# Causal attentions: q and k as 32-row fp32r strips instead of bf16 parts copied through DRAM

## What is computed

```
qkv = x @ W;  att = q k^T / 4;  att = where(causal, -1e9, att)
out = softmax(att) @ v @ W_out                      # sublayers 0 and 4
scores = (q k^T) * tril;  out = softmax(scores / 32) @ v @ Wo   # sublayer 6
```

## Time and profile before

| | us |
|---|---|
| runs | 1302.36, 1304.68, 1298.7 |
| profiled execution, span | 1298.8 |
| PE busy | 1006.1 (77%) |
| DVE busy | 816.7 (63%) |
| ACT busy | 472.6 (36%) |
| POOL busy | 253.6 (20%) |
| largest group, maxima on DVE (L954, 576) | 284.3 |
| largest on PE, scores for maxima (L1374, 576) | 182.2 |

### The profile page before, as it was taken

One profiled execution on the slowest core, in us unless ns is written; L12 is line 12 of the kernel. 1 busy time (PEld: TensorE's weight loads), 2 busy tenths in 40 slices (PEclk: granted clock), 3 DMA queues, 4 the chain that ended last, 5 costly groups with the idle time before them and its releaser, 6 DMA issues.

```text
span 1298.8 us, 16170 instructions
## 1 busy us (share of the span) xinstructions
PE 1006.1 (77%) x5870; PEld 561.0 (43%) x5870; DVE 816.7 (63%) x1958; ACT 472.6 (36%) x1041; POOL 253.6 (20%) x378
## 2 busy tenths in 40 slices
PE   5469998789137877689999645999967469999785
PEld 3124443674125554443736421444444124443575
DVE  4558883767139999453232635888768468885566
ACT  1115565431038876221011110555612104557232
POOL 4000000333028776200000300000198000000033
PEclk8669999889659897689999975999967669999788
DMA  7950000101580000020000197200001970000000
GB/s 261 153 69 2 2 2 1 33 1 23 108 175 22 1 2 1 1 96 1 1 0 1 49 146 97 99 2 2 2 0 49 152 91 2 2 2 1 1 1 33
DMA packets 18907, 54.69 MB, mean 42 GB/s; under 512 B 2065, under 2 KB 3633, under 8 KB 17804
## 3 DMA queue, kind: packets, MB, share of 16 engines
q1 hardware_dynamic: 18828, 53.65, 20.9%
HBM read 40.90 MB, written 12.45 MB: 41 GB/s over the span
## 4 chain that ended last, share of the span: by engine, by line
PE 51%; DVE 29%; issue 10%; DMA 5%; ACT 4%; SPq 1%; POOL 1%; DVEq 0%; POOLq 0%; ACTq 0%
PE bank L1284 8%; PE bank L1374 8%; PE pair L1284 6%; PE pvb L1418 6%; DVE pmx L954 5%; PE pair L1401 5%; PE bank L1622 4%; DVE nm L1077 3%; PE bank L1576 3%; DMA scratch<-parts 3%; ACT PB L698 2%; PE pair L1289 2%; DVE PB L1089 2%; DVE rest L1192 2%; DMA QO<-scratch 2%
## 5 line engine op out<-in xcount | busy, mean ns | idle before, releaser
L954 DVE TENSOR_REDUCE pmx<-bank 128x1 f32<-128x512 f32 (+3 forms) x576 | 284.3, 551 | 121.8 <-PE bank L1377 94.7
L698 ACT ACTIVATE PB<-pair 128x1024 f32<-128x1024 f32 (+3 forms) x288 | 225.0, 812 | 289.1 <-PE pair L1404 246.3
L1374 PE MATMUL bank<-KO,QO 96*128 96x512 bf16 (+3 forms) x576 | 182.2, 366 | 66.8 <-issue 51.0
L1401 PE MATMUL pair<-QO,KO 99*128 99x512 bf16 (+3 forms) x576 | 152.9, 332 | 33.1 <-issue 31.1
L1374 PEld LDWEIGHTS bank<-KO,QO 96*128 96x128 bf16 x576 | 55.3, 101 | 205.2 <-DVE pmx L954 100.1
L1418 PE MATMUL pvb<-PB,V 128*32 128x512 f32 (+3 forms) x1152 | 124.0, 501 | 0.0
L1487 PE MATMUL pair<-KO,QO 96*128 96x192 bf16 x256 | 60.5, 280 | 75.8 <-DMA QO<-scratch 48.9
L735 ACT ACTIVATE KO<-pair,nm 128x192 f32<-128x192 f32 x216 | 87.8, 422 | 79.3 <-DVE nm L1077 77.5
L577 POOL TENSOR_TENSOR QO_r<-rest,acc 128x512 fp32r<-128x512 f32 x16 | 21.3, 1332 | 462.5 <-DVE acc L1198 462.5
L1077 DVE TENSOR_REDUCE nm<-pair 128x2 f32<-128x384 f32 x128 | 65.0, 545 | 48.7 <-PE pair L1489 48.1
L836 DVE TENSOR_TENSOR X<-bank,X 128x256 f32<-128x256 f32 x56 | 23.7, 423 | 105.4 <-PE bank L1622 43.9
(11 more groups left out here) (216 smaller groups left out, 1726.6 us busy)
## 6 DMA issues: line engine op xcount, KB each, us to landing
scratch<-parts SPq DMA_DIRECT2D x14, 768.0 KB, 11.8
QO<-scratch SPq DMA_DIRECT2D x36, 256.0 KB
KO<-scratch SPq DMA_DIRECT2D x36, 256.0 KB
WF<-in_moe_gu SPq DMA_DIRECT2D x1, 3520.0 KB, 27.9
WA<-in_w_att SPq DMA_DIRECT2D x3, 1024.0 KB, 10.6
QO<-scratch SPq DMA_DIRECT2D x24, 128.0 KB
WF<-in_tern_w SPq DMA_DIRECT2D x1, 3072.0 KB, 10.2
V<-in_moe_d SPq DMA_DIRECT2D x1, 1792.0 KB, 8.5
```

Of the source, the lines that this page charges most:

```text
L698: act.activation(pb[:, st % 2, 2 * i:2 * i + 2, 0:n], ps[:, :, 0:n], ACT.Exp, scale=scale)\
L954: r_done(dve.tensor_reduce(pmx[:, g % 2, c, t, j:j + 1], ps[:, 0:n], AX.X, ALU.max))
L1374: last = pe.matmul(ps[:, 0:n], q_op[0:KROWS, h, t * P:(t + 1) * P], k_op[0:KROWS, h, c * HALF:c * HALF + n], start=True, stop=not diag)
L1401: last = pe.matmul(ps[:, j, 0:n], k_op[0:KROWS + 3, h, kb * P:(kb + 1) * P], q_op[0:KROWS + 3, h, q0:q0 + n], start=True, stop=not diag)
```

## The change

q and k are no longer split in bf16 parts. The weights of q and k arrive with each head's 16 columns doubled (`both`), so that the projection gives 32 rows per head, four heads on 128 partitions. q becomes one strip per head: rows 0 to 15 the value rounded to fp32r, rows 16 to 31 the rest (two ScalarE copies with scales from `strip_sv`, and a subtraction on POOL, which makes the sign come out). k becomes two operands, the rounded value and its rest, each in both halves. A score is two fp32r matmuls over 32 rows. The maximum, in two fp32r terms, is added by a third one against ones. Everything stays in SBUF; `replicate`, `maxima` and their DMAs are gone for the causal attentions. There are 16 projections of 512 columns per attention instead of 8, spread over the plan ("k", "q" items).

The causal mask leaves TensorE: for the maxima VectorE adds it while it reduces (`maximum`), for the exponentials POOL sets the forbidden triangle of exp(scores) to zero (`causal_half`), and the product with V waits for it. Maxima are now computed two heads at a time; such a pair can ride in an "exp" item, on the other two strips, its matmuls between those of the exponentials. `HEAD_START` counts 10 items, pairs now. The transposes of the maxima go to a double bank and ScalarE copies them. The ternary weights of the last sublayer are prepared on POOL partly between its new work.

```diff
-HEAD_START = 18
+HEAD_START = 10
 def max_units(g, qh):
 
-    units = [(("max", g, t, c, j), 60 + min((t + 1) * P - c * HALF, HALF))
-             for t in range(qh * TH, (qh + 1) * TH) for c in range(1 + qh) for j in range(HG)]
-    return units + [(("m", g, qh), 600)]
+    units = [(("max", g, t, c, jj), 2 * (60 + min((t + 1) * P - c * HALF, HALF)))
+             for t in range(qh * TH, (qh + 1) * TH) for c in range(1 + qh) for jj in range(2)]
+    units.append((("m", g, qh), 600))
+    n = len(STAGES)
+    k = STAGES.index((g, qh)) + 1
+    if 1 < k < n:
+        at = len(units) // 2
+        units[at:at] = [((side,) + STAGES[k], 0) for side in ("k", "q")]
...
+    plan = [("k", 0, 0), ("q", 0, 0)] + [("v", t) for t in range(TH)] + [("x1",), ("k", 0, 1), ("q", 0, 1)] \
+        + [("v", t) for t in range(TH, NT)]
     ahead = [(item, cost, n) for n, stage in enumerate(STAGES) for item, cost in max_units(*stage)]
...
@@ -186,11 +200,17 @@
                     for m in range(len(STAGES)) if ahead and m >= ahead[0][2]], default=0)
         for i in range(2):
             lead += rate / 2
+            if i == 0 and g == 0:
+                plan += [("suffix", t) for t in (NT - 1 - 2 * k, NT - 2 - 2 * k) if t >= 0]
+            with_exp = None
+            if ahead and lead > 0 and ahead[0][0][0] == "max":
+                if ahead[1][0][0] == "max" and ahead[0][0][4] == i and ahead[0][0][:4] == ahead[1][0][:4]:
+                    ahead[0], ahead[1] = ahead[1], ahead[0]
+                with_exp, cost, _ = ahead.pop(0)
+                lead -= cost
+            plan.append(("exp", g, qh, kb, i, with_exp))
             while ahead and lead > 0:
                 lead -= take()
-            if i == 0 and g == 0:
-                plan += [("suffix", t) for t in (NT - 1 - 2 * k, NT - 2 - 2 * k) if t >= 0]
-            plan.append(("exp", g, qh, kb, i))
             if (g, qh, i) == (NG - 1, 1, 1):
...
+            def causal_half(s, item):
+
+                _, g, qh, kb, i, _ = item
+                pool.wait_ge(e_free, e_after(s, item))
+                p2 = pb[:, STEP[g, qh, kb] % 2, 2 * i:2 * i + 2, 0:P]
+                pool.affine_select(p2, p2, pattern=[[0, 2], [1, P]], compare_op=ALU.is_ge, fill=0.0, base=0,
+                                   channel_multiplier=-1).then_inc(causal, 1)
+
+            def strip(s, n, item):
+
+                side, g, half = item
+                cols = slice(half * HALF, (half + 1) * HALF)
+                pool.wait_ge(e_free, e_after(s, item))
+                if side == "q":
+                    ins = pool.tensor_tensor(qs[:, g, cols], y_f[:, n % 2, :], h_r[:, n % 2, :].bitcast(F32), ALU.subtract)
+                else:
+                    ins = pool.tensor_tensor(ks[1][:, g, cols], y_f[:, n % 2, :], ks[0][:, g, cols].bitcast(F32),
+                                             ALU.subtract)
+                ins.then_inc(strip_ready, 1)
+
...
+                    if item[0] in ("k", "q"):
+
+                        side, g, half = item
+                        cols = slice(half * HALF, (half + 1) * HALF)
+                        ps = e_slot()[:, 0, :]
+                        if strips >= 2:
+
+                            act.wait_ge(strip_ready, strips - 1)
+                        y = y_f[:, strips % 2, :]
+                        if side == "q":
+                            act.activation(y, ps, ACT.Copy, scale=strip_sv[:, 0:1])
+                            act.activation(h_r[:, strips % 2, :], ps, ACT.Copy, scale=strip_sv[:, 1:2]).then_inc(e_free, 1)
+                        else:
+                            act.activation(y, ps, ACT.Copy)
+                            act.activation(ks[0][:, g, cols], ps, ACT.Copy).then_inc(e_free, 1)
+                        strips += 1
+                    if item[0] == "mT":
 
                         _, g, qh = item
-                        ts = slice(qh * TH, (qh + 1) * TH)
-                        act.wait_ge(mp_ready, 2 * (NG * a + g) + qh + 1)
-                        act.activation(em[:, g % 2, ts, :], nm[:, g % 2, ts, :], ACT.Exp, scale=scale)\
...
+            def maximum(g, t, c, j):
+
+                n = min((t + 1) * P - c * HALF, HALF)
+                ps = r_slot()
+                to = pmx[:, g % 2, c, t, j:j + 1]
+                if (t + 1) * P - c * HALF <= HALF:
+                    r_done(dve.tensor_tensor_reduce(junk[:, (r_used - 1) % 3, 0:n], ps[:, 0:n], tri[:, HALF - n:HALF], 1.0, LOWEST,
+                                                    ALU.add, ALU.max, accum_out=to))
+                else:
+                    r_done(dve.tensor_reduce(to, ps[:, 0:n], AX.X, ALU.max))
 
...
-                        dve.wait_ge(mrow_ready, n + 1)
-                        dve.nop().then_inc(r_free, 1)
+                            dve.wait_ge(e_free, e_after(s, ("mT",) + STAGES[n - 2]))
+                        top, low = (nms_r[:, n % 2, :, k:P:STRIP] for k in range(2))
+                        step(dve.tensor_copy(top, nm[:, b, ts, :]))
+                        dve.tensor_tensor(low, nm[:, b, ts, :], top.bitcast(F32), ALU.subtract).then_inc(mp_ready, 1)
                     if item[0] == "accT":
                         _, g, qh = item
                         t0 = qh * TH
...
+                        unit = item if item[0] == "max" else item[5]
+                        if unit:
+                            _, gm, t, c, jj = unit
+                            if (c, t % TH, jj) == (0, 0, 0):
+                                pe.wait_ge(strip_ready, len(STRIPS) * a + STRIPS.index(("q", gm, t // TH)) + 1)
+                            nx = min((t + 1) * P - c * HALF, HALF)
+                            px = [r_slot()[:, 0:nx] for _ in range(2)]
+                        if item[0] == "exp":
+                            _, g, qh, kb, i, _ = item
+                            if kb == i == 0:
+
+                                pe.wait_ge(e_free, e_after(s, ("mT", g, qh)))
+                                if (s, g, qh) == (0, 0, 0):
+                                    pe.wait_ge(v_blank, 2)
+                            q0, n = span(qh, kb)
+                            b = STAGES.index((g, qh)) % 2
+                            ps = e_slot()
+                        for part in range(3):
+                            for j in range(2 if item[0] == "exp" else 0):
+                                if part < 2:
+                                    last = scores(ps[:, j, 0:n], ks[part][:, g, kb * P:(kb + 1) * P], qs[:, g, q0:q0 + n],
+                                                  2 * i + j, part == 0, False)
+                                else:
+                                    rows = slice((2 * i + j) * STRIP, (2 * i + j) * STRIP + 2)
+                                    at = q0 - qh * HALF
+                                    last = pe.matmul(ps[:, j, 0:n], ones_r[rows, :], ms[rows, b, at:at + n],
+                                                     start=False, stop=True)
+                            if part == 2 and item[0] == "exp":
+                                last.then_inc(e_full, 1)
+                                e_at[g, qh, kb] = e_used
+                            for j in range(2 if unit and part < 2 else 0):
+                                last = scores(px[j], qs[:, gm, t * P:(t + 1) * P], ks[part][:, gm, c * HALF:c * HALF + nx],
+                                              2 * jj + j, part == 0, part == 1)
+                                if part:
+                                    last.then_inc(r_full, 1)
                     if item[0] == "pv":
                         _, g, qh, kb = item
                         st = STEP[g, qh, kb]
...
 
                             pe.wait_ge(acc_ready, ACC0[s] + 2 * g + qh)
                         pe.wait_ge(e_free, e_at[g, qh, kb])
+                        if (g, qh, kb, 1) in DIAGS:
+                            pe.wait_ge(causal, len(DIAGS) * a + DIAGS.index((g, qh, kb, 1)) + 1)
                         for j in range(HG):
                             last = pe.matmul(pvb[j * STRIP:(j + 1) * STRIP, q0 - qh * HALF:HALF],
...
     down = np.concatenate([g["L1_ffn_down_w"].transpose(0, 2, 1).reshape(-1, D), g["L1_ffn_sh_down_w"].T,
                            np.zeros((NF_MOE * P - F_MOE, D), np.float32)], 0)
+
+    def both(wq, wk):
+
+        w = np.stack([chunks(w).reshape(P, ND, NG, HG, HD) for w in (wq, wk)], 1)
+        w = w.transpose(0, 3, 1, 2, 4, 5)
+        return np.ascontiguousarray(np.broadcast_to(w[:, :, :, :, :, None, :], (P, NG, 2, ND, HG, DUP, HD))
+                                    .reshape(P, NG, 2, ND, P))
+
+    w0, w2 = g["L0_attn_w_project"].T, g["L2_attn_w_qkv"]
...
```

363 lines of the change are left out of this document (166 added, 197 removed).

## The result

| | before | after |
|---|---|---|
| median of four runs, us | 1300.5 | 1500.1 (1478.0 to 1513.3) |
| ratio, 95% interval | | 1.146, 1.136 to 1.157 |
| profiled execution, span | 1298.8 | 1476.3 |
| mean granted clock | 0.866 | 0.796 |
| PE busy | 1006.1 | 1187.5 |

The kernel is 15% slower. The ratio leaves out the two runs of after that took over 1.5% more than its fastest one (1500.3 and 1513.3), so it is smaller than the quotient of the medians. The prediction, 1290 us in a range of 1240 to 1352, was wrong. The rest became 91.6 us shorter, as forecast; the third phases became 269 us longer where 85.5 were forecast.

A forecast was written before the change was run, and what follows sets the result against it. DMA and latency were taken to bound the first two phases, TensorE the third. -98 + 3 x 28.5 = -12.5 us on the 1298.8 span gives 1286.3; the median lies 3.6 higher, so 1290, range 1240 to 1352.

The forecast's parts named there:

- third phases: Each causal attention from its first exponential step on, bound by TensorE; forecast to grow by 28.5 us each.
- Phases one and two: Projection, then first maxima, before the first exponential step of each causal attention: 98 us saved in all, bounds 85 to 110.
- The strips run together: Third phase: matmuls on different strips of 32 rows were assumed to run with full concurrency, a 512 column round costing 0.23 us.
- the rival of strips in turn: Third phase: strips run one after another, 97 us more per attention less vanished waits, about 1520 us; chance 0.04.
- The clock: Third phase: rounds priced at 2.4 columns per ns, the 2.4 GHz level, where the granted clock was 0.97 before.
- TensorE's work, "32.4 to 36.8, minus 2": Third phase, us per group of four heads: 32.4 before, 36.8 after (+4.4), minus 2 for rounds of alternating strips overlapping.
- Bank wait: Third phase: a pair of maxima following another waits for VectorE to free its bank; 0.5 us x 10 per group, +5.
- The slower rival: Bank wait costs the full 0.8 us, +35 us, so 1325; with dear accumulator read or select 1345; chance 0.31.
- Read of the accumulator: VectorE's separate read after each diagonal maximum, third phase: 0.1 us, bounds 0 and 0.2, counted in the bank wait's 0.5.
- ScalarE: Third phase: its added copies, 24 us per attention against 60.7 of 108 busy, were forecast to be hidden.
- Select: POOL's mask on exponentials, third phase: 0.7 us each, bounds 0.455 and 1.33; waits 3 us per attention, bounds 0 and 12.
- the forecast's own sign: Wrong if first exponential steps aren't some 30 us earlier per attention, or the third phase grows under 15 or over 40.

The follow-up runs named there:

- experiments 1, 2 and 6: 1: before, score matmuls reading 32/64 rows, 1671.1/1607.9 us; 2: after, strip matmuls over 128 rows/one strip, 1602.0/2094.7; 6: after, third matmul over 32/128 rows, 1418.3/1493.5.
- experiment 7: After, with the third matmul of each score reading 32 rows and VectorE reading only the last 128 columns of each bank: 1351.0 us, ratio 1.037.
- experiment 4: After, with VectorE reading only the last 128 columns of each bank (short reduction): 1402.5 us; the same with strip matmuls over 128 rows: 1558.3.

## Why the prediction was wrong, step by step

- **Phases one and two: right.** First maximum at 30.6 us (31.5 forecast); 12 us after V is blanked in the second attention (13) and 12 after the last normalisation ahead of the third (12). Saved 22.6, 34.2 and 34.1 us, 91 in all (98, bounds 85 to 110). What fell short is the way from the first maximum to the first exponential step, 30.6, 31.0 and 32.3 us where 25 was forecast, at a clock of 0.61.
- **The strips run together: right.** All four start at 219.69; the rival of strips in turn is not what happened. Made real, it costs 2095 us and not 1520, mostly since its working, too, kept the full clock; with 128 rows, at a clock of 1.00 in the third phases, turns cost 1602, still 82 above it.
- **The clock: the step that failed most.** The forecast priced every round at 2.4 columns per ns and never wrote down that the earlier trace rows show 0.97 for matmuls that read 96, 99 and 128 rows. The change puts matmuls of 32 and 2 rows in place of those of 96 and 99. About 119 of the 183 us that the third phases exceed their forecast are this: the cause is shown by experiments 1, 2 and 6, the size is an estimate. None of the rivals had it.
- **TensorE's work, "32.4 to 36.8, minus 2": too low.** It made 5 to 6 us per attention without waits, and experiment 7 leaves some 24. A round of four strips holds 0.31 us and not 0.23, since its weights arrive no earlier, and a step ends with 0.35 to the next work. A step of 512 columns is 0.31 + 0.23 + 0.35 = 0.89; the forecast had 0.72. Were all 96 steps that far off, it would be 16 us, most of the difference; the rest was not traced. A part is a slip in adding: the terms of before, 7.7 + 7.7 + 3.8 + 9.4 + 1.2 + 2.0, make 31.8 and not 32.4, so "+4.4" should be +5.0, 2.4 us per attention. The Trainium skill ("TensorE: Matmul & The Clock Gate", part 3 on packing, "Measured speedup vs the span model") gives 3.07 times for four, from which 0.30 per round is an estimate. The trace's 0.31 to the second round agrees with it, its 0.23 to the third doesn't. I had named the 0.30 and decided against it, and had priced it wrongly: 135,500 columns are 265 rounds of 512, and 0.07 more for each is 18 us per attention, not 6. The same part of the Trainium skill says that a weight load runs beside a matmul in flight only if that is on other rows. The trace doesn't agree: in the 45 places the loads for the same strips start 0.08 after the first round and end at 0.29, and the second round starts at 0.31.
- **Bank wait: right in kind and near in size.** Forecast 0.5 us in 39 places, 20 per attention. At the high level a riding pair of 512 columns behind another waits 1.04 - 0.35 = 0.69; what the short reduction takes away is 8 to 12 us per attention without the clock (experiment 4). With the reads cut the clock rose too, which doubled the gain (74 us in the phases, 38 of them clock). The slower rival had this mechanism and 1325 to 1345; the size of the loss was not its.
- **Read of the accumulator, ScalarE: right. Select: below its bounds.** The read takes 0.08 and is hidden, ACT is busy for 97 of 233 us. The select takes 0.41, under the forecast's lower bound of 0.455, and no run resolves what is left of its wait.

In all, with 119 for the clock, 108 for what experiment 7 leaves (36 x 3: 71 work, 37 idle) and 42 for the rest, which the shorter reads took: -91.6 + 119 + 108 + 42 = +177, the difference of the two spans. Beside the forecast of the third phases, 85.5 us: TensorE's work 71 where it had 16.5, waits 79 (37 + 42) where it had 69, clock 119 where it had nothing. The 42 is what is left over in the sum, so the split is an estimate; it is borne out by TensorE's idle time, 67 us more than before. The forecast's size of the waits was good; its work was short by a factor of four, and the clock was missing. By the forecast's own sign (third phases longer by over 40 us) it was wrong: they grew by 93, 85 and 90.

## What to carry to other kernels

Before work on TensorE is cut into narrow row tiles, look at the granted clock of the stretch and ask which rows its matmuls read: the same columns took nearly twice the time at 32 rows as at 96 (264 against 140 us for the phase), although TensorE was busy for 263 of the 264 us. Where an operand has spare rows that are zero, let the matmul read them: 30 rows of zeros in the third round of each step were worth 72 to 82 us. And price a round of row tiles from start to start, new weights included, not by its columns.
